# Dispatch of a layer of experts: no clearing between the transfers of its first three parts, and the third ranking moved ahead

## The reference

```python
score = relu(xf @ rw1 + rb1) @ rw2 + rb2          # 8 scores a token
_, topi = top_k(score, 2)
mask = zeros(...).at[arange(T)[:, None], topi].set(True)
gate = softmax(where(mask, score, -inf))
for e in range(8):
    h = relu(xf @ W1[e] + b1[e])                  # 128 -> 512
    y = h @ W2[e] + b2[e]                         # 512 -> 128
    out = out + gate[:, e:e + 1] * y
x = x + gb * out
```

## Time and profile before

| what | us |
|---|---|
| median of three executions | 522.41 |
| the three | 522.19, 524.29, 522.41 |
| the profiled execution, its own time | 523.29 |
| its span, from the first to the last instruction | 521.6 |

### The profile page before, as it was taken

How to read it: one execution, slowest core, us unless ns; L and a number is a source line. 1 busy time by engine, 2 the same in 40 slices (tenths; PEclk the granted TensorE clock), 3 DMA queues, 4 the chain that set the end, 5 groups by cost and what they waited for, 6 DMA issues and landing times.

```text
span 521.6 us, 16754 instructions
## 1 busy us (share of the span) xinstructions
PE 448.8 (86%) x5323; PEld 353.6 (68%) x5323; DVE 372.6 (71%) x1026; ACT 348.2 (67%) x1521; POOL 369.9 (71%) x586
## 2 busy tenths in 40 slices
PE   6979898888888888888799996778797889999977
PEld 5555666666666666666554436677696779999977
DVE  6775999999999999999847664745541435555754
ACT  3673999999999999999857542433262658666900
POOL 6973675555778767878626878886888887777640
PEclk9997999999999999999989996979888999999979
DMA  8461000000000220030230131223322222225355
GB/s 205 123 177 42 12 13 13 14 13 13 13 13 13 55 74 11 13 93 14 88 102 30 45 92 46 80 87 92 90 74 75 65 75 78 80 73 171 102 145 189
DMA packets 61519, 36.54 MB, mean 70 GB/s; under 512 B 25806, under 2 KB 57334, under 8 KB 61306
## 3 DMA queue, kind: packets, MB, share of 16 engines
q1 hardware_dynamic: 55834, 25.83, 19.0%
q0 software_dynamic: 4352, 9.45, 5.4%
q10 hardware_dynamic: 1248, 0.20, 0.2%
HBM read 20.56 MB, written 14.88 MB: 68 GB/s over the span
## 4 chain that ended last, share of the span: by engine, by line
PE 27%; DVE 24%; ACT 23%; issue 13%; another core or an unknown queue 6%; DVEq 2%; POOL 2%; DMA 1%; SPq 0%; ACTq 0%; POOLq 0%
ACT pr L1034 21%; DVE nmax L1101 8%; PE pAm L1954 7%; PE pScm L1962 4%; PE pSpm L1962 3%; PE pAm L1494 2%; PE pScm L1264 2%; DVE oT L947 1%; DVE w1t L1814 1%; DVEq L1569 1%; DMA x_all<-in_L_attn_x 1%; PE pScm L1509 1%; ACT act L1721 1%; DVE stat L1346 1%
## 5 line engine op out<-in xcount | busy, mean ns | idle before, releaser
L1034 ACT ACTIVATE pr<-pS,nmax 128x136 f32<-128x136 f32 x512 | 185.0, 380 | 13.5 <-DVE nmax L1101 13.3
L1721 ACT ACTIVATE act<-pAm,w1t 128x128 f32<-128x128 f32 x288 | 82.0, 372 | 79.8 <-remote 36.6
L1034 ACT ACTIVATION_READ_ACCUMULATOR pr<-pS,nmax 128x1 f32 x512 | 108.6, 212 | 0.0
L1954 PE MATMUL pAm<-hgT,w1t 128*128 128x128 f32 x576 | 84.9, 292 | 14.0 <-DVE w1t L1814 6.2
L1063 PE MATMUL pS<-kT,qbd 64*128 64x136 f32 x1024 | 93.8, 302 | 1.5 <-ACT pr L1034 1.2
L1666 POOL DMA_INDIRECT y_scr<-ys,si x72 | 72.1, 1001 | 25.2 <-DVE ys L1830 13.2
L1101 DVE TENSOR_REDUCE nmax<-pS 128x4 f32<-128x544 f32 x128 | 87.8, 686 | 2.1 <-PE pS L1067 1.4
L1954 PEld LDWEIGHTS pAm<-hgT,w1t 128*128 128x128 f32 x576 | 76.3, 205 | 17.5 <-issue 9.5
L1109 DVE STREAM_TRANSPOSE prT<-pr 128x640 f32<-128x640 f32 x96 | 81.1, 845 | 8.7 <-ACT pr L1034 0.2
L1063 PEld LDWEIGHTS pS<-kT,qbd 64*128 64x128 f32 x1024 | 68.3, 186 | 14.5 <-ACT pr L1034 1.1
L1631 POOL DMA_INDIRECT xs<-h_all,pos_i x64 | 64.8, 1012 | 11.2 <-issue 9.7
(11 more groups left out here) (304 smaller groups left out, 708.3 us busy)
## 6 DMA issues: line engine op xcount, KB each, us to landing
hg<-xs SPq DMA_DIRECT2D x72, 72.0 KB
vbd<-v_scr SPq DMA_DIRECT2D x132, 16.0 KB, 1.8
v_scr<-h_all SPq DMA_DIRECT2D x8, 256.0 KB, 2.5
h_all<-y_scr SPq DMA_DIRECT2D x8, 256.0 KB, 2.9
w_all<-y_scr SPq DMA_DIRECT2D x8, 256.0 KB, 4.8
x_all<-in_L_attn_x SPq DMA_DIRECT2D x3, 512.0 KB, 6.8
w_all<-in_L_ffn_W SPq DMA_DIRECT2D x2, 768.0 KB, 4.9
w_all<-in_L_ffn_W SPq DMA_DIRECT2D x3, 512.0 KB, 6.0
```

The source lines that it names most:

```text
L1034: e.activation(pr[:, n, to:to + SPAN], scored(j, gi)[:, lo:lo + SPAN], ACT.Exp, bias=nmax[:, k:k + 1], scale=-1.0, accum_out=rs[u][:, k:k ...
L1721: e.activation(ac(u)[:, k, :], pU[u % W][:, k, :], ACT.Relu, bias=w1t[u // 2 % 4][:, u % 2, FF + D + k:FF + D + k + 1]).then_inc(a_up.sem, 1)
L1954: mm = e.matmul(pU[u % W][:, k, :], w1t[u // 2 % 4][:, u % 2, k * P:(k + 1) * P], hgT[u // 2 % 4][:, u % 2, :], start=True, stop=True)
```

## The change

There are three edits. GpSimd leaves out the clearing after each of the 32 transfers of parts 0, 1 and 2 (`CLOSE = 3`); parts 3 and 4 and the scatters keep theirs. TensorE ranks part 2 at the start of group 6, ahead of the transposes of group 7, instead of in the middle of group 6. VectorE places part 2 ahead of the scores of group 4 instead of behind them.

```diff
@@ group_of_router(e, g)
+                if g == 6:
+                    ranked(e, 2)
                 if g + 1 < NG:
                     turned_rows(e, g + 1)
                 hidden(e, g, 0)
...
                 if g >= 4:
                     summed(e, g - 2)
-                if g == 6:
-                    ranked(e, 2)
                 hidden(e, g, 1)
@@ route_gpsimd(e)
+                CLOSE = 3
                 sent = 0
                 for p, (first, end) in enumerate(PARTS):
                     routed(e, p)
                     for r in range(2 * first, 2 * end):
                         dispatch(e, r // 2, r % 2)
-                        breath()
+                        if p >= CLOSE:
+                            breath()
@@ route_vector(e)
                 choose_both(e, 2)
+                place(e, 2)
                 token_scores(e, 4)
-                place(e, 2)
                 all_listed(1)
```

## The result

The changed kernel took 547.48 us (median of 4 runs, 544.9 to 549.82), the kernel before 523.35 in the same comparison: 1.044 times the time, 95% interval 1.040 to 1.049. It is slower by 24 us where 1.6 us of gain were forecast. The profiled execution took 549.82.

The account below looks back on a forecast made before the run. Three engines waiting for each other from 299 to 325 us were taken as the bound there. Clearings 0 and ranking and place 1.6 us off 523.29 gave 521.7 us profiled, a median of 520.8, range 517.5 to 524.5.

Parts of the forecast that it names:

- What bounds the kernel: From 299 to 325 us three engines wait for each other; from 430 to 486 us TensorE is the bound.
- its loose end: Three waits for TensorE end 1.46, 2.74 and 2.64 us after its rows end; no row names a cause.
- The clearings: Leaving out 0.31 us clearings gives back some 0.09 us per transfer, 1.4 us per 16; costed at nothing by itself.
- Part 2 earlier, the load of tile 8 earlier: GpSimd ends part 2's transfers 4.1 us earlier; SyncE's load of tile 8 moves from 330.83 to about 326.7.
- Ranking and place: Place of part 2 ends 4.7 us earlier, in idle VectorE time, at no added wait; 1.6 us of gain taken.
- The 2.4 us: Last router scores at about 314.2 instead of 316.56 if ScalarE's last copy is released at once; two thirds taken.
- The wall that the prediction named: Scores of group 7 need ScalarE's copy of the last `partial`, which hangs on ScalarE's chain, not VectorE; gain possibly nothing.
- Nothing: Rival: ScalarE's copy at 314.12 stays and the earlier transfers are hidden; 522.2 us, chance 0.26.
- The slower rival: VectorE's eight matrix copies, 313.8 to about 330 us, each wait 0.5 us for transfers: 4.0 us, 524.8 us; chance 0.16.
- The largest unknown: TensorE's unexplained waits between 336 and 430 us may change with GpSimd's new timing, several us either way.

Follow-up runs that it names:

- e8: Kernel before with 340 instead of 240 columns cleared after the transfers of parts 0 to 2, order as before: 524.05 us, 0.999.
- e1: Kernel before without the clearings of parts 0 to 2, order of ranking and place as before: 543.97 us, 1.032.
- e3: Kernel before with 8 instead of 240 columns cleared after the transfers of parts 0 to 2: 544.07 us, 1.041.
- e16: The changed kernel, unchanged, run again on a chip where the kernel before took 502.04 us: 501.28 us, 0.997.
- e15: The kernel before, no edit, traced on the same chip as the rerun of the changed kernel: 507.09 us in one run.
- e2: Kernel before with only ranking and place of part 2 moved as in the change, all clearings kept: 527.17 us, 1.002.
- e13: The changed kernel's order with all clearings kept and 340 columns in each, against the kernel before: 517.06 us, 1.023.
- e17: Kernel before with 340 columns in every clearing, as e10, run on the chip of e15 and e16: 516.78 us, 1.028.
- e12: Kernel before with 340 columns in the clearings, but 240 behind the last part: 513.11 us, 1.016.
- e10: Kernel before with 340 instead of 240 columns in every clearing, order as before: 512.3 us, 0.979.
- e4: Kernel before with 480 instead of 240 columns cleared after the transfers of parts 0 to 2: 528.55 us, 1.013.
- e7: Kernel before without the clearings of part 2 alone, order as before: 539.07 us, 1.032.
- e9: Kernel before with clearings of one partition instead of 128 in the first three parts, 240 columns as before: 523.36 us, 1.000.
- e5: Kernel before with eight no-operations on GpSimd in place of each clearing of the first three parts: 544.53 us, 1.038.
- e6: Kernel before without the clearings of parts 0 and 1, those of part 2 and later kept: 528.18 us, 1.008.

## Why the prediction was wrong

**What bounds the kernel: right, and its loose end was the answer.** The three engines do wait for each other between 299 and 325 us. The prediction saw three releases late by 1.46 to 2.74 us, wrote that no row names a cause, and went on. They were late because of GpSimd's transfers: at a pitch of 1.54 us or more, or on chip C, such waits are all but gone (e8 has two left, of 0.9 and 1.4 us).

**The clearings: the step that failed.** The prediction says "this edit is costed at nothing, and it protects the others". Leaving the clearings out costs 3.2% by itself (e1), and 4.1% where a distance as short is kept with tiny ones (e3): 17 to 21 us of the 24. What it looked at was GpSimd's time only; the clearing's work for the others, a distance between transfers, had no term. The rest of the loss is within the intervals of these runs. The size of the pitch was off too: 1.36 us was taken from the last scatters, and 1.27 was measured, so a clearing takes 0.18 us of GpSimd's time and not 0.09. Whether 1.36 us would have cost as much is not known, as nothing between 1.29 and 1.43 us was tried.

**Part 2 earlier, the load of tile 8 earlier: wrong.** The prediction said that only GpSimd's own queue holds it. But GpSimd waited 6.86 us for place of part 2, 8.84 for that of part 3 and 20.23 for that of part 4; SyncE's next loads started at 336.94 in place of 330.83. Where signals are prompt the step holds: on chip C these loads start 44.7 us behind the first transfer with the change (e16) and 52.0 without it (e15), 7.3 us earlier, where 4.1 were forecast.

**Ranking and place: mechanism right, worth nothing.** Place runs 0.5 us behind the ranking in the changed kernel, as forecast (in e2, where the ranking's signal was late, 2.7 us). The gain of 1.6 us was not seen: e2 shows 1.002 (0.996 to 1.007), too wide to exclude it, but with prompt signals the router's stretch is 38.81 us with the new order (e13) against 38.76 and 38.77 with the old (e17, e12). The 2.4 us that the sum took two thirds of were to come if ScalarE's copy was released at once. Promptness alone gives that, with the old order: e10's stretch is 38.78 us against 41.84, and the order adds nothing to it. The wall that the prediction named, ScalarE's chain of `partial` copies, holds whether releases are late or not. For this part alone, the rival *Nothing* comes nearest.

**The slower rival: right sign, wrong mechanism.** It let VectorE's copies of matrices wait for transfers, 4 us. Most of the loss was there ahead of them, in waits for TensorE, and it was five times as large. In the changed kernel's trace the copies came after part 2 had ended. On chip C they did meet transfers back to back (e16):

```profile
309.63 1.21 POOL L1631 DMA_INDIRECT xs<-h_all,pos_i  x1 [0.30 <-issue]
```

```profile
310.23 0.50 DVE L1816 COPY w1t<-w_all 128x644 f32 x1 [0.32 <-issue]
```

The copy starts inside the transfer and takes its usual 0.50 us after a usual gap (0.33 us between copies elsewhere); the transfer takes 1.21 us instead of 0.97. So the transfer grew, as in the earlier trace rows, and the copies' waits that this rival feared are not seen.

**The largest unknown.** "TensorE's waits between 336 and 430 us" did grow: the stretch from the first products to the end took 211.9 us against 201.5 in the two profiled executions, 10 of the 26.5 us between them. Part of it are the late results of 345 to 354 us and part 4's transfers behind them, as shown above; but single traces vary by several us here (208.8 us in e2, which is no slower than before). The prediction called it several us either way, and neither the range nor the chances took it in.

**Small slips.** The copies of matrices between 313.8 and 330.6 us are seven and not eight, which makes that rival's price 3.5 us by its own rule. *Nothing* is given as 522.2 us where the median is 522.4, and 520.8 + 7.8 is 528.6 and not 528. None of them changes the forecast.

**What stays open.** That a short pitch of GpSimd's indirect transfers makes TensorE's signals late on chips A and B is shown by e3, e4, e7, e8, e9 and e10. Why it does, and why not on chip C, is not; nor was it separated whether GpSimd's instruction counts or the traffic that the transfer starts. The pitch is not all that counts either: at 1.45 us and more a signal was 8.7 us late in part 3 of the changed kernel, where the router of before has at most 2.7. Whether the first comparison ran on A, on B or on a chip like them is not recorded; its times of before (522 to 528 us) are theirs. Nor is it known whether the difference belongs to the chips or to what else went on beside them at the time.

## What to carry to other kernels

A release that comes later than its producer's row ends was no noise here: find what runs at those times before changing it, and price an instruction between two transfers by the distance that it gives the others, too. Try such a distance in steps, for it can be too short and too long: on chips A and B 1.45 us was too dense, 1.54 us everywhere gave 2.1%, and 1.66 us in the last parts made GpSimd's queue the bound. And compare on more than one chip before a distance is tuned: on chip C the same 340 columns cost 2.8% and the change nothing.

## What the runs showed of the hardware

- TensorE's signals reached VectorE and ScalarE up to 13.7 us after the last matmul's row ended, while GpSimd issued indirect transfers every 1.27 us (the changed kernel; e1, e3, e5 and e7 on chip A); some of the waits end 1.9 to 2.8 us after it stops, others while its transfers go on. At 1.45 us the largest lateness in the router was 2.7 to 3.7 us, but 8.7 us behind it in the changed kernel; at 1.54 us it was 1.4 us in e8 and under 0.1 in e10's router.
- On chip C they came at once at 1.27 us too, and the kernel before took 502 to 507 us instead of 524.
- An indirect transfer takes 0.97 us on GpSimd and 0.30 us of gap; eight no-operations between two of them add nothing, a clearing of 8 columns adds 0.02 us at most (0.12 to 0.13 and 0.18 in place of 0.30), one of 240 columns 0.18 us, whatever its partitions (0.29 us on 1, 0.31 on 128).
- Executions of kernels that don't differ up to there, on one chip, fall into two groups some 5 us apart at GpSimd's first transfer (near 273 or near 278 us; on chip A e3 273.06 and e6 278.48, on chip C e16 273.27 and e15 277.24); single traces are compared from a common event, not by their absolute times.
